# Flipped half tiles through DRAM in five transfers each, and two late features looked up from on-chip tables (recommender tower, one core)

## The chip, the cores and the metric

The kernel runs on one core of one Trainium2 chip. The metric is the device time of one execution in microseconds (us); less is better. The profile is one execution recorded by the hardware profiler.

## The reference

27 embedding tables are read by the ids of 2048 samples; all pairwise dot products of the 27 rows, with 16 dense inputs, go through three layers.

```python
e = jnp.stack([tbl_0[ids[:, 0]], ..., tbl_26[ids[:, 26]]], axis=1)   # (2048, 27, 128)
interactions = jnp.einsum('bnd,bmd->bnm', e, e)
i, j = jnp.triu_indices(27, k=1)
z = interactions[:, i, j]                                          # (2048, 351)
h = jnp.concatenate([z, dense_ctx], axis=1)                        # (2048, 367)
h = jnp.maximum(h @ W_top1 + b_top1, 0.0)                          # 512
h = jnp.maximum(h @ W_top2 + b_top2, 0.0)                          # 256
y = h @ W_top3
```

Tables have 1000, 1250, 12500 or 125000 rows. Those of features 24 and 25 have 1000.

## The kernel before

The samples are worked in 8 pairs p of tiles (t = 0, 1) of 128 samples each; a "cycle" below is the work of one pair on TensorE (PE). The product stage needs `emb` with the embedding dimension on the partitions, [dimension, tile, sample, feature]. Features get there in two ways.

**One-hot features** (11, each with 1000 rows). Their tables stay in SBUF in two rounded parts, `table_hi` and `table_lo`, 125 partitions by 8 chunks. VectorE (DVE) compares broadcast ids (`ids_b`) with row numbers and writes a "piece" of 125x2048 (`make_onehot`, line 798; a ring of 3 pieces). PE multiplies 16 times per piece pair: `look_up`, lines 625 and 627. ScalarE (ACT) takes the sums to `emb` and, for lookups that serve two pairs, to `held` (lines 923 and 924; placed one pair later by line 936). The set of 5 features is looked up in cycles 0, 2, 4, 6 and the set of 6 in cycles 1, 3, 5, always for two pairs at once (two pieces for a lookup; 8 matmuls of 512 columns per piece). Cycle 7 looks up 6 for itself alone, with one piece of 16 matmuls of 256 columns each.

**Gathered features** (16). GpSimd (POOL) issues one indirect DMA per feature and tile (line 596) into `rows`, a ring of 5 banks of 4 features. A tile has 4 banks n = 0 to 3. In pairs 1 to 7, three of the four half tiles (two banks each) are "flipped": DVE transposes 32x32 blocks (`flip_half`, line 853) into `flips`, SyncE's queue (SP) moves the blocks between partitions by DMA into `moved` (`move_half`, line 415: 4x4 transfers of 32 partitions by 1 KB, all issued one after another), and ACT copies `moved` to `emb` (`take_half`, line 955). The fourth half tile (t = 1, n = 2, 3) is transposed on PE (`turn`, line 636) between the products of tile 0 and layer 2.

`flips` and `moved` are single buffers. `flip_half` waits until the transfers of the half before have landed (line 848). `move_half` waits until its own half is flipped and until ACT has placed the half before (line 412).

**PE's order in cycle p**: the lookups of p; layer 1 of pair p-1 (`layer1`, line 672); products of tile 0 (`gram_products`, line 655); the two turned banks; layer 2 of p-1 (line 681); products of tile 1. After cycle 7 come the last pair's layers (`last_layers`).

**DVE's order in cycle p**: pieces 0, 1, 2; flip (p,0,0); the scores of p-2 (`score`, which wait for layer 2 in cycle p-1); piece 3; flip (p,0,1); pieces 4 to 7; flip (p,1,0); the rest of the pieces. In cycle 7 there are 6 pieces and the last flip follows them. The first part of this runs ahead, during PE's cycle p-1.

**ACT's order in cycle p**: place held; take half (p,0,0); take the lookups, with half (p,0,1) before the fifth; layer 1's four tiles; half (p,1,0); the products of tile 0; the two turned banks; the products of tile 1.

**SP's order in cycle p** (lines 515 to 532): up to two loads of ids, each of which waits until the piece of four lookups earlier is made; the four stores of the products of p-1 (line 440); move (p,0,1); the three loads of z (line 479), which wait for these stores; dense and ids; move (p,1,0); ids; move (p+1,0,0); store y. Products go out to DRAM in one layout and come back as z in another.

SP issues every one of these in this written order; a wait in it holds all that follows.

Of the kernel before, what the change touches and what calls it, by code (L numbers as in the profile page):

```python
# [31 lines left out]
F32 = mybir.dt.float32  # L32
# [5 lines left out]
P = 128  # L38
# [22 lines left out]

SETS = [list(range(NO // 2)), list(range(NO // 2, NO))]
HELD = max(len(features) for features in SETS)
LOOKUPS = [(0, 0, 2), (1, 0, 1), (1, 1, 2), (0, 2, 2), (1, 3, 2), (0, 4, 2), (1, 5, 2), (0, 6, 2), (1, 7, 1)]
IDS_SLOTS = 4


def emb_slot(k):
    return NG + k


def held_place(k):

    return k - SETS[1][0] if k in SETS[1] else k

# [11 lines left out]
def bank_features(p, n):  # L87

    end = min((n + 1) * TURNS_A_BANK, NG)
    return n * TURNS_A_BANK, end - n * TURNS_A_BANK  # L90
# [135 lines left out]
def build(nc, dense_t, ids_rows, ids_onehot, gathered_tables, onehot_tables, w1, w2, w3, b1, b2, out):  # L226
    with ExitStack() as ctx:
# [40 lines left out]
        products = nc.dram_tensor("products", (2, DRAM_ROWS, NF, QUARTERS, RUN), F32)  # L268

        last_products = nc.dram_tensor("last_products", (TILES, DRAM_ROWS, NF, QUARTERS, GROUPS), F32)  # L270

# [49 lines left out]
        turned = sem("turned")  # L321
        flipped = sem("flipped")
        half_moved = sem("half_moved")
        half_placed = sem("half_placed")
        emb_taken = sem("emb_taken")
        gram_full = sem("gram_full")
# [38 lines left out]

        HALF_MOVED = BLOCKS * BLOCKS * 16

# [23 lines left out]
        def _(sp):  # L391
            def load_ids(i):

                _, k, p0, pairs, _ = LOOKUP_LIST[i]
                if i - NO >= IDS_SLOTS:

                    sp.wait_ge(onehot_ready, pieces_by(i - IDS_SLOTS))
                slot = (i - NO) % IDS_SLOTS
                width = pairs * PAIR
                sp.dma_start(ids_b[:, slot, 0:width], ids_onehot[k:k + 1, p0 * PAIR:p0 * PAIR + width]  # L400
                             .rearrange("k b -> (k b)").partition_broadcast(P)).then_inc(ids_loaded[slot], 16)

            def lookups_of(p):
                return [i for i, lookup in enumerate(LOOKUP_LIST) if lookup[0] == p]

            def move_half(p, t, h):

                number = HALF_NUMBER[(p, t, h)]
                sp.wait_ge(flipped, FLIPPED_BY[(p, t, (h + 1) * HALF_BANKS - 1)])

                if number > 0:
                    sp.wait_ge(half_placed, number)
                for q in range(BLOCKS):
                    for b in range(BLOCKS):
                        sp.dma_start(  # L415
                            moved[b * BLOCK:(b + 1) * BLOCK, q, :, :].rearrange("p f j -> p (f j)"),
                            flips[q * BLOCK:(q + 1) * BLOCK, b, :, :, :].rearrange("p g f j -> p (g f j)")
                        ).then_inc(half_moved, 16)

# [88 lines left out]
            for dst, src in ((w1_sb[:], w1), (w2_sb[:], w2)):  # L508
                sp.dma_start(dst, src).then_inc(weights_loaded, 16)
            load_dense(0)  # L510
            for i in lookups_of(1)[:IDS_SLOTS]:
                load_ids(i)
            move_half(1, 0, 0)
# [88 lines left out]
        def _(pe):  # L602
# [7 lines left out]
            def look_up(i):  # L610
                _, k, p0, pairs, piece = LOOKUP_LIST[i]
                ps = free_emb_bank(("look", i))
                if i < NO:
                    pe.wait_ge(table_split, (k + 1) * GRAM_BANKS)
                chunks = ROWS_PER // pairs
                width = pairs * PAIR
                for part in range(pairs):
                    pe.wait_ge(onehot_ready, piece + part + 1)
                    if shared_onehot(i) and part == pairs - 1:

                        pe.wait_ge(onehot_rest, i + 1)
                    columns = onehot[0:ROWS, (piece + part) % ONEHOT_RING, :].rearrange("p (j b) -> p j b", b=width)
                    for c in range(chunks):
                        j = part * chunks + c
                        nc.tensor.matmul(ps[:, 0:width], table_hi[0:ROWS, k, j, :], columns[:, c, :],  # L625
                                         start=j == 0, stop=False)
                        last = nc.tensor.matmul(ps[:, 0:width], table_lo[0:ROWS, k, j, :], columns[:, c, :],  # L627
                                                start=False, stop=j == ROWS_PER - 1)
                    last.then_inc(onehot_read, 1)
# [145 lines left out]
        def _(dve):  # L775
# [67 lines left out]
            def flip_half(p, t, h):  # L843

                number = HALF_NUMBER[(p, t, h)]
                if number > 0:

                    dve.wait_ge(half_moved, number * HALF_MOVED)
                for g in range(HALF_BANKS):
# [4 lines left out]
                                        row_bank(p, t, n).rearrange("p f (b i) -> p f b i", b=BLOCKS)  # L854
                                        ).then_inc(flipped, 1)

            for p in range(1, PAIRS):
# [23 lines left out]
        def _(act):  # L881
# [66 lines left out]
            def take_half(p, t, h):  # L948
# [7 lines left out]
                               moved[:, :, 0:size, :].rearrange("d q f j -> d q j f")).then_inc(half_placed, 1)  # L956

            def take_gram(p, t):
                if t == 0 and p > 0:
# [42 lines left out]
            for p in range(PAIRS):  # L1002
# [21 lines left out]
                chunk = (p - 1) * MLP_CHUNKS  # L1024
                if p > 0:
                    for m in range(M1):
                        take_layer1(chunk, m)
                    take_half(p, 1, 0)
# [70 lines left out]
```

## Time and profile before

| | us |
|---|---|
| median of 3 runs | 444.68 (444.11 to 446.41) |
| the profiled execution, own time | 444.69 |
| its span, first to last instruction | 442.9 |
| TensorE busy | 341.5 (77%) |
| DVE busy | 246.3 (56%) |
| POOL busy | 242.6 (55%) |
| ACT busy | 199.4 (45%) |
| mean granted clock of TensorE | 0.903 of full |

Busy time leaves out DMA issue: SP's work is seen only in the chain that ended last, in the waits and in the timeline of its queue. In timeline rows the first number is the start in us from the beginning of the span, the second the duration; an idle time with what ended it stands in brackets. A row of windows gives the stretch, its length, the busy time (and instructions) of PE, PE's weight loads, DVE, ACT and POOL, then TensorE's granted clock as a share of full, the busy share of the DMA engines and GB/s. The starts of PE's cycles, T1 to T7, are where the first lookup of the pair runs.

### The profile page before, as it was taken

The numbers are of one execution on the slowest core, as the hardware profiler recorded it, in microseconds if no ns is written. First come the engines' busy times: TensorE is split into PE (matmuls) and PEld (weight loads), VectorE is DVE, ScalarE is ACT, GpSimd is POOL, SyncE is SP. The second block draws the span as 40 slices with busy tenths as digits, with TensorE's granted clock in tenths as the row PEclk, the third lists the DMA queues.
The fourth block names the chain that finished last, engine by engine and source line by source line (L and its number), as shares of the span: only waits on it lengthen the run. The fifth ranks groups of instructions, "written<-read, shape, count | busy, mean of one in ns | idle before, by whom it ended". The sixth has DMA issues, their size and how long they took to land.

```text
span 442.9 us, 8208 instructions
## 1 busy us (share of the span) xinstructions
PE 341.5 (77%) x3310; PEld 281.3 (64%) x3310; DVE 246.3 (56%) x202; ACT 199.4 (45%) x294; POOL 242.6 (55%) x263
## 2 busy tenths in 40 slices
PE   3999893759994989629896789809899489718767
PEld 2677793547872877428774678508786379717666
DVE  6899964596185726459266925739247743610100
ACT  5798663125463257113572166212662256322432
POOL 6777777660577637753377727754177737720000
PEclk9999998869999799959999699958999699867889
DMA  7966825562274536754174645844246533732230
GB/s 184 217 163 195 227 76 149 157 152 79 77 176 129 145 91 83 200 126 134 53 166 123 161 99 73 207 113 134 68 105 174 140 79 83 176 89 55 44 62 14
DMA packets 70111, 55.09 MB, mean 124 GB/s; under 512 B 45186, under 2 KB 60111, under 8 KB 70073
## 3 DMA queue, kind: packets, MB, share of 16 engines
q1 hardware_dynamic: 60121, 37.56, 35.4%
q0 software_dynamic: 8192, 16.79, 15.0%
q8 instruction: 26, 0.43, 0.4%
q10 hardware_dynamic: 1760, 0.22, 0.3%
q14 instruction: 12, 0.10, 0.1%
HBM read 36.43 MB, written 7.09 MB: 98 GB/s over the span
## 4 chain that ended last, share of the span: by engine, by line
SPq 45%; PE 30%; issue 10%; DMA 6%; DVE 5%; ACT 3%; ACTq 1%; DVEq 0%
SPq L415 31%; SPq L440 8%; PE emb_ps L625 7%; PE emb_ps L627 6%; PE mlp_ps L672 6%; DVE onehot L798 4%; PE gram_ps L655 4%; DMA moved<-flips 3%; DMA h<-tbl_rows 2%; PE mlp_ps L681 2%; SPq L400 2%; ACT emb L955 2%; PE emb_ps L699 1%; SPq L479 1%; DVE flips L853 1%
## 5 line engine op out<-in xcount | busy, mean ns | idle before, releaser
L596 POOL DMA_INDIRECT rows<-tbl_rows,idx x256 | 241.7, 944 | 147.5 <-issue 74.1
L625 PE MATMUL emb_ps<-onehot,table_hi 125*128 125x512 f32 (+1 forms) x400 | 158.0, 404 | 68.9 <-DVE onehot L798 59.5
L798 DVE TENSOR_TENSOR onehot<-ids_b,row_id 125x2048 fp32r<-125x2048 int32 x72 | 160.0, 2273 | 42.7 <-PE emb_ps L627 32.4
L627 PE MATMUL emb_ps<-onehot,table_lo 125*128 125x512 f32 (+1 forms) x400 | 152.1, 389 | 0.0
L625 PEld LDWEIGHTS emb_ps<-onehot,table_hi 125*128 125x128 f32 x400 | 82.5, 206 | 96.4 <-issue 59.1
L627 PEld LDWEIGHTS emb_ps<-onehot,table_lo 125*128 125x128 f32 x400 | 82.7, 207 | 13.0
L655 PE MATMUL gram_ps<-emb 128*54 128x54 f32 x2048 | 58.1, 216 | 11.2 <-ACT gram L966 10.2
L655 PEld LDWEIGHTS gram_ps<-emb 128*54 128x54 f32 x2048 | 54.9, 132 | 17.4 <-ACT gram L966 11.1
L955 ACT COPY emb<-moved 128x1024 f32<-128x1024 f32 x21 | 42.3, 2016 | 45.1 <-DMA moved<-flips 45.0
L853 DVE STREAM_TRANSPOSE flips<-rows 128x512 f32<-128x512 f32 x42 | 27.3, 689 | 62.0 <-DMA moved<-flips 62.0
L923 ACT COPY held<-emb_ps 128x256 f32<-128x256 f32 x38 | 14.2, 375 | 105.3 <-PE emb_ps L627 105.1
L966 ACT COPY gram<-gram_ps 118x432 f32<-118x432 f32 x64 | 32.5, 519 | 40.5 <-PE gram_ps L655 38.5
L672 PE MATMUL mlp_ps<-z,w_sb 126*128 126x256 f32 x168 | 40.3, 399 | 10.6 <-DMA z<-products 10.6
L672 PEld LDWEIGHTS mlp_ps<-z,w_sb 126*128 126x128 f32 x168 | 33.7, 201 | 16.2 <-DMA z<-products 10.8
L835 DVE TENSOR_TENSOR mlp_ps<-mlp_ps,rows 128x256 f32<-128x256 f32 x14 | 6.1, 433 | 65.4 <-PE mlp_ps L681 65.4
L924 ACT COPY emb<-emb_ps 128x256 f32<-128x256 f32 x50 | 33.7, 688 | 5.8 <-PE emb_ps L627 5.8
L798 DVE TENSOR_TENSOR onehot<-z,mlp_ps 125x2048 fp32r<-125x2048 int32 (+1 forms) x16 | 33.5, 2116 | 1.5 <-PE mlp_ps L726 1.1
L681 PE MATMUL mlp_ps<-w_sb,h 128*128 128x256 f32 x112 | 25.3, 379 | 0.0
L975 ACT ACTIVATE h<-mlp_ps,columns 128x256 f32<-128x256 f32 x28 | 13.3, 474 | 24.1 <-PE mlp_ps L672 24.1
L681 PEld LDWEIGHTS mlp_ps<-w_sb,h 128*128 128x128 f32 x112 | 20.7, 190 | 2.5
L936 ACT COPY emb<-held 128x1280 f32<-128x1280 f32 (+1 forms) x7 | 19.2, 2739 | 0.2
L945 ACT COPY emb<-emb_ps 128x512 f32<-128x512 f32 x22 | 13.6, 652 | 0.1
(51 smaller groups left out, 129.0 us busy)
## 6 DMA issues: line engine op xcount, KB each, us to landing
moved<-flips SPq DMA_DIRECT2D x336, 32.0 KB
ids_b<-ids_onehot SPq DMA_DIRECT2D x33, 256.0 KB, 4.7
products<-gram SPq DMA_DIRECT2D x28, 216.0 KB
gram<-tbl_rows SPq DMA_DIRECT2D x9, 480.0 KB
rows<-tbl_rows,idx POOLq DMA_INDIRECT x256
z<-products SPq DMA_DIRECT2D x14, 126.0 KB
h<-tbl_rows SPq DMA_DIRECT2D x2, 480.0 KB
z<-products SPq DMA_DIRECT2D x7, 112.0 KB
```

Of the source, the lines that this page charges most:

```text
L415: sp.dma_start(moved[b * BLOCK:(b + 1) * BLOCK, q, :, :].rearrange("p f j -> p (f j)"), flips[q * BLOCK:(q + 1) * BLOCK, b, :, :, :].rearr ...
L440: sp.dma_start(products[p % 2, to:to + STORE_ROWS, :, q, :], gram[row:end, q % ABREAST, :, :]).then_inc(products_out, 16)
L596: pool.indirect_dma_start(out=rows[:, bank_number(p, t, n) % ROW_BANKS, f - first, :], out_offset=None, in_=gathered_tables[f], in_offset= ...
L625: nc.tensor.matmul(ps[:, 0:width], table_hi[0:ROWS, k, j, :], columns[:, c, :], start=j == 0, stop=False)
L627: last = nc.tensor.matmul(ps[:, 0:width], table_lo[0:ROWS, k, j, :], columns[:, c, :], start=False, stop=j == ROWS_PER - 1)
L655: last = nc.tensor.matmul(ps[half * HALF_ROWS:half * HALF_ROWS + GRAM_COLS, b * GRAM_COLS:(b + 1) * GRAM_COLS], samples, samples, start=Tr ...
L672: last = nc.tensor.matmul(ps[:, 0:PAIR], w1_sb[0:k, s, m * P:(m + 1) * P], z[0:k, s, :], start=s == 0, stop=s == STEPS - 1)
L681: last = nc.tensor.matmul(mlp_ps[t][:, 0:HID2], h1[:, k, t * P:(t + 1) * P], w2_sb[:, k, :], start=k == 0, stop=k == M1 - 1)
L798: nc.vector.tensor_tensor(onehot[0:ROWS, seq % ONEHOT_RING, 0:own * width].rearrange("p (j b) -> p j b", b=width), *operands, ALU.is_equal ...
L924: nc.scalar.copy(emb[:, :, :, emb_slot(k)], ps[:, 0:PAIR].rearrange("d (t b) -> d t b", t=TILES)).then_inc(emb_taken, 1)
L955: nc.scalar.copy(emb[:, t, :, first:first + size].rearrange("d (q j) f -> d q j f", j=BLOCK), moved[:, :, 0:size, :].rearrange("d q f j -> ...
L966: nc.scalar.copy(gram[0:GRAM_PART, :, :, g0:g0 + GROUPS_A_BANK].rearrange("r s j g -> r (s j) g"), gram_ps[a % GRAM_BANKS][0:GRAM_PART, 0: ...
```

## The change

1. `move_half` is split. `store_half` waits for the flip and writes the whole of `flips` (128 partitions by 4 KB) to a DRAM tensor `halves` in one transfer. `load_half` waits for that transfer to land and for ACT to have placed the half before, and reads `moved` back with four transfers of 32 partitions by 4 runs of 1 KB. `flip_half` now waits for the store of the half before, no longer for `moved`. `halves` has two places. In SP's order the store of (p,0,1) stands before the loads of z and its load behind them; (p,1,0) has one load of ids between store and load; (p+1,0,0) has nothing between.
2. Features 24 and 25, the last two gathered ones, are looked up one-hot for pairs 6 and 7. Bank 3 of these tiles shrinks from 4 features to 2. Cycle 6 gets two more lookups (4 pieces). Their tables go into the places of one-hot tables 0 and 1 after the last lookup of those: SP loads each through `h1` as stage (`load_late_table`), ACT rounds it (`round_late`), DVE forms the low part (`split_late`). SP loads table 1 only after the split of table 0. Their ids come from `ids_rows`, copied within DRAM by four transfers of 4-byte elements near the start (`store_late_ids`).

```diff
+LATE_FEATURES = [24, 25]
+LATE_SLOT = GATHERED.index(LATE_FEATURES[0])
+LATE_PAIR = PAIRS - 2
...
+LATE_SPLITS = [6, 9]
 HALF_AFTER = 4
+LATE_ROUNDS = [2, 4]
...
+            def store_half(p, t, h):
+                sp.wait_ge(flipped, FLIPPED_BY[(p, t, (h + 1) * HALF_BANKS - 1)])
                 number = HALF_NUMBER[(p, t, h)]
-                sp.wait_ge(flipped, FLIPPED_BY[(p, t, (h + 1) * HALF_BANKS - 1)])
+                sp.dma_start(halves[number % 2], flips[:, :, :, :, :].rearrange("p b g f j -> p b (g f j)")
+                             ).then_inc(half_stored, 16)
+
+            def load_half(p, t, h):
+                number = HALF_NUMBER[(p, t, h)]
+                sp.wait_ge(half_stored, (number + 1) * 16)
                 if number > 0:
                     sp.wait_ge(half_placed, number)
-                for q in range(BLOCKS):
-                    for b in range(BLOCKS):
+                for b in range(BLOCKS):
+                    sp.dma_start(moved[b * BLOCK:(b + 1) * BLOCK, :, :, :].rearrange("p q f j -> p q (f j)"),
+                                 halves[number % 2, :, b, :].rearrange("(q p) x -> p q x", p=BLOCK)
+                                 ).then_inc(half_moved, 16)
+            def store_late_ids():
+                for n in range(len(LATE)):
+                    for t in range(TILES):
                         sp.dma_start(
+                            late_ids[n:n + 1, :].rearrange("k (p t b) -> t (k p) b", t=TILES, b=P)[t],
+                            ids_rows[LATE_PAIR:PAIRS, :, :].rearrange(
+                                "a p (t f) -> f t a p", t=TILES)[LATE_SLOT + n, t],
+                            allow_slow_non_contiguous=True).then_inc(late_ids_stored, 16)
+            def load_late_table(n):
+                if n == 0:
+                    sp.wait_ge(mlp_full, (LATE_PAIR - 1) * MLP_CHUNKS)
+                else:
+                    sp.wait_ge(late_split, n)
...
             for p in range(1, PAIRS):
+                if p == LATE_PAIR:
+                    load_late_table(0)
                 for i in ids[0:2]:
                     load_ids(i)
                 store_products(p - 1)
-                move_half(p, 0, 1)
+                store_half(p, 0, 1)
+                if p == LATE_PAIR:
+                    load_late_table(1)
                 load_z(p - 1)
+                load_half(p, 0, 1)
                 load_dense(p)
...
-                move_half(p, 1, 0)
-                for i in ahead[2:]:
+                store_half(p, 1, 0)
+                for i in ahead[2:3]:
+                    load_ids(i)
+                load_half(p, 1, 0)
+                for i in ahead[3:]:
                     load_ids(i)
                 if p < LAST:
-                    move_half(p + 1, 0, 0)
+                    store_half(p + 1, 0, 0)
+                    load_half(p + 1, 0, 0)
                     store_y(p - 1)
...
                 if number > 0:
-                    dve.wait_ge(half_moved, number * HALF_MOVED)
+                    dve.wait_ge(half_stored, number * 16)
...
+            def split_late(n):
+                dve.wait_ge(late_rounded, n + 1)
+                nc.vector.tensor_tensor(table_lo[...], late_stage, table_hi[...].bitcast(F32), ALU.subtract
+                                        ).then_inc(late_split, 1)
...
+                    if p == LATE_PAIR and at in LATE_SPLITS:
+                        split_late(LATE_SPLITS.index(at))
                     make_onehot(i, part)
...
+            def round_late(n):
+                act.wait_ge(late_loaded, (n + 1) * 16 * len(TABLE_PARTS))
+                act.wait_ge(onehot_read, pieces_by(cycle_lookups(LATE_PAIR)[n]))
+                nc.scalar.copy(table_hi[...], late_stage).then_inc(late_rounded, 1)
...
                     if p > 0 and at == HALF_AFTER:
                         take_half(p, 0, 1)
+                    if p == LATE_PAIR and at in LATE_ROUNDS:
+                        round_late(LATE_ROUNDS.index(at))
```

## Rows read from the trace of the kernel before

**Rows 1.** The chain that ended last, as shares of the span, by engine and line.

```profile
SPq 45%; PE 30%; issue 10%; DMA 6%; DVE 5%; ACT 3%; ACTq 1%; DVEq 0%
SPq L415 31%; SPq L440 8%; PE emb_ps L625 7%; PE emb_ps L627 6%; PE mlp_ps L672 6%; DVE onehot L798 4%; PE gram_ps L655 4%; DMA moved<-flips 3%; DMA h<-tbl_rows 2%; PE mlp_ps L681 2%; SPq L400 2%; ACT emb L955 2%; PE emb_ps L699 1%; SPq L479 1%; DVE flips L853 1%
```

**Rows 2.** Windows: cycles 1 to 7 and the tail (columns: see the section on the profile).

```profile
62.40:121.00 58.60, 43.58 (x401) 35.99 (x400) 32.08 (x24) 21.15 (x31) 32.11 (x35) 0.88 0.45 121
121.00:168.00 47.00, 38.88 (x389) 31.41 (x385) 27.78 (x22) 21.50 (x30) 30.02 (x32) 0.93 0.54 134
168.00:223.50 55.50, 41.73 (x403) 33.84 (x401) 31.99 (x24) 21.78 (x31) 30.11 (x33) 0.88 0.53 119
223.50:270.10 46.60, 38.90 (x388) 31.50 (x384) 27.78 (x22) 21.30 (x29) 30.18 (x33) 0.93 0.55 135
270.10:326.20 56.10, 42.06 (x405) 34.03 (x401) 31.99 (x24) 21.74 (x31) 30.47 (x33) 0.88 0.52 118
326.20:373.00 46.80, 38.54 (x387) 31.13 (x385) 27.78 (x22) 21.30 (x29) 29.94 (x32) 0.93 0.49 120
373.00:423.60 50.60, 34.03 (x404) 30.98 (x400) 11.23 (x13) 18.76 (x24) 13.50 (x15) 0.80 0.37 87
423.60:442.90 19.30, 12.03 (x74) 10.79 (x70) 0.98 (x4) 4.12 (x12) 0.00 (x0) 0.91 0.21 40
```

**Rows 3.** Timeline of SP's queue, cycles 3 and 4.

```profile
172.85 7.01 SPq L440 DMA_DIRECT2D products<-gram  x4
179.96 11.20 SPq L415 DMA_DIRECT2D moved<-flips  x16
...
225.69 4.86 SPq L440 DMA_DIRECT2D products<-gram  x4
230.65 10.40 SPq L415 DMA_DIRECT2D moved<-flips  x16
241.14 2.58 SPq L479 DMA_DIRECT2D z<-products  x3
```

**Rows 4.** Timeline of DVE, cycles 3 and 4.

```profile
192.89 1.30 DVE L853 STREAM_TRANSPOSE flips<-rows 128x512 f32<-128x512 f32 x2 [10.46 <-DMA moved<-flips]
...
229.14 8.84 DVE L798 TENSOR_TENSOR onehot<-ids_b,row_id 125x2048 fp32r<-125x2048 int32 x4
242.36 1.30 DVE L853 STREAM_TRANSPOSE flips<-rows 128x512 f32<-128x512 f32 x2 [4.38 <-DMA moved<-flips]
```

**Rows 5.** Timeline of PE: starts of matmuls in cycle 4, and its layer 1.

```profile
226.35 0.39 PE L625 MATMUL emb_ps<-onehot,table_hi 125*128 125x512 f32 x1
226.57 0.39 PE L627 MATMUL emb_ps<-onehot,table_lo 125*128 125x512 f32 x1
...
245.98 0.77 PE L625 MATMUL emb_ps<-onehot,table_hi 125*128 125x512 f32 x1 [5.83 <-DVE onehot L798]
...
252.30 5.36 PE L672 MATMUL mlp_ps<-z,w_sb 126*128 126x256 f32 x24
```

**Rows 6.** Windows within cycle 4, before and after PE's idle time that ends at 245.98.

```profile
224.00:240.00 16.00, 15.27 (x63) 11.16 (x62) 12.27 (x7) 8.09 (x9) 12.27 (x13) 1.00 0.66 158
246.00:251.20 5.20, 5.20 (x12) 4.12 (x13) 4.61 (x3) 0.00 (x0) 3.98 (x5) 0.50 0.77 196
```

**Rows 7.** Timeline of POOL in cycle 4: two gathers, the first behind a turned bank.

```profile
263.20 0.94 POOL L596 DMA_INDIRECT rows<-tbl_rows,idx  x1 [6.97 <-PE emb_ps L636]
264.45 0.94 POOL L596 DMA_INDIRECT rows<-tbl_rows,idx  x1 [0.31 <-issue]
```

**Rows 8.** DMA landings: ids of 256 KB (source view of line 400) and `moved` (chain).

```profile
DMA to landing us min/median/max: 3.8/4.5/10.2
...
407.79 2.67 DMA moved<-flips
```

**Rows 9.** Groups by form (busy us, mean ns): low parts of tables, halves taken.

```profile
L819 DVE TENSOR_TENSOR table_lo<-gram,gram_ps 125x512 fp32r<-125x512 f32 x18 | 11.5, 681 | 1.1 <-ACT gram_ps L896 1.1
L955 ACT COPY emb<-moved 128x1024 f32<-128x1024 f32 x21 | 42.3, 2016 | 45.1 <-DMA moved<-flips 45.0
```

More of the change, by code:

```diff
@@ L58 @@
 ONEHOT_RING = 3
-SETS = [list(range(NO // 2)), list(range(NO // 2, NO))]
-HELD = max(len(features) for features in SETS)
-LOOKUPS = [(0, 0, 2), (1, 0, 1), (1, 1, 2), (0, 2, 2), (1, 3, 2), (0, 4, 2), (1, 5, 2), (0, 6, 2), (1, 7, 1)]
+LATE_FEATURES = [24, 25]
+LATE_SLOT = GATHERED.index(LATE_FEATURES[0])
+LATE_PAIR = PAIRS - 2
+LATE = [NO + n for n in range(len(LATE_FEATURES))]
+SETS = [list(range(NO // 2)), list(range(NO // 2, NO)), LATE]
+LOOKUPS = [(0, 0, 2), (1, 0, 1), (1, 1, 2), (0, 2, 2), (1, 3, 2), (0, 4, 2), (1, 5, 2), (0, 6, 2),
+           (2, LATE_PAIR, 2), (1, 7, 1)]
+HELD = len(LATE) + len(SETS[0])
 IDS_SLOTS = 4
 def emb_slot(k):
-    return NG + k
+    return NG + k if k < NO else LATE_SLOT + k - NO
 def held_place(k):
-    return k - SETS[1][0] if k in SETS[1] else k
+    first = SETS[1][0] if k in SETS[1] else LATE_SLOT - NG
+    return (k if k < NO else emb_slot(k) - NG) - first
 EMB_BANKS = 3
@@ L87, in bank_features @@
 def bank_features(p, n):
-    end = min((n + 1) * TURNS_A_BANK, NG)
+    end = min((n + 1) * TURNS_A_BANK, LATE_SLOT if p >= LATE_PAIR else NG)
     return n * TURNS_A_BANK, end - n * TURNS_A_BANK
@@ L268, in build @@
         products = nc.dram_tensor("products", (2, DRAM_ROWS, NF, QUARTERS, RUN), F32)
+        halves = nc.dram_tensor("halves", (2, P, BLOCKS, HALF_BANKS * TURNS_A_BANK * BLOCK), F32)
+        late_ids = nc.dram_tensor("late_ids", (len(LATE), 2 * PAIR), I32)
+        late_stage = h1[0:ROWS, :, :].rearrange("p m b -> p (m b)")
         last_products = nc.dram_tensor("last_products", (TILES, DRAM_ROWS, NF, QUARTERS, GROUPS), F32)
@@ L322, in build @@
         flipped = sem("flipped")
+        half_stored = sem("half_stored")
         half_moved = sem("half_moved")
         half_placed = sem("half_placed")
+        late_ids_stored = sem("late_ids_stored")
+        late_loaded = sem("late_loaded")
+        late_rounded = sem("late_rounded")
+        late_split = sem("late_split")
         emb_taken = sem("emb_taken")
@@ L399, in load_ids @@
                 width = pairs * PAIR
-                sp.dma_start(ids_b[:, slot, 0:width], ids_onehot[k:k + 1, p0 * PAIR:p0 * PAIR + width]
-                             .rearrange("k b -> (k b)").partition_broadcast(P)).then_inc(ids_loaded[slot], 16)
+                if k >= NO:
+                    sp.wait_ge(late_ids_stored, len(LATE) * TILES * 16)
+                    ids = late_ids[k - NO:k - NO + 1, :]
+                else:
+                    ids = ids_onehot[k:k + 1, p0 * PAIR:p0 * PAIR + width]
@@ L420, in load_dense @@
+            def load_late_table(n):
+                if n == 0:
+                    sp.wait_ge(mlp_full, (LATE_PAIR - 1) * MLP_CHUNKS)
+                else:
+                    sp.wait_ge(late_split, n)
+                table = gathered_tables[LATE_SLOT + n].rearrange("(p j) d -> p (j d)", j=ROWS_PER)
+                for p0, p1 in TABLE_PARTS:
+                    sp.dma_start(late_stage[p0:p1, :], table[p0:p1, :]).then_inc(late_loaded, 16)
             def load_dense(p):
@@ L614, in look_up @@
                     pe.wait_ge(table_split, (k + 1) * GRAM_BANKS)
+                if k in LATE:
+                    pe.wait_ge(late_split, k - NO + 1)
+                table = k % NO
                 chunks = ROWS_PER // pairs
@@ L624, in look_up @@
                         j = part * chunks + c
-                        nc.tensor.matmul(ps[:, 0:width], table_hi[0:ROWS, k, j, :], columns[:, c, :],
+                        nc.tensor.matmul(ps[:, 0:width], table_hi[0:ROWS, table, j, :], columns[:, c, :],
                                          start=j == 0, stop=False)
-                        last = nc.tensor.matmul(ps[:, 0:width], table_lo[0:ROWS, k, j, :], columns[:, c, :],
+                        last = nc.tensor.matmul(ps[:, 0:width], table_lo[0:ROWS, table, j, :], columns[:, c, :],
                                                 start=False, stop=j == ROWS_PER - 1)
@@ L1025, in _ @@
                 if p > 0:
+                    if p == LATE_PAIR:
+                        act.wait_ge(late_split, len(LATE))
                     for m in range(M1):
```

17 lines of the change are left out of this document (11 added, 6 removed).

## The prediction

> **What bounds the kernel now.** I read the chain that ended last first [rows 1]. SP's queue holds 45% of it, and the block transfers of line 415 alone 31%: the path runs through the issue of small transfers, more than through arithmetic. Next come the windows by cycle [rows 2]. TensorE is busy 39 to 44 us of each cycle of 47 to 58 us, at a granted clock of 0.88 to 0.93. So there are idle stretches, and a clock that falls with them. SP's timeline shows their source [rows 3]: in cycle 4 the stores of products take until 230.55, the 16 transfers of half (4,0,1) start only then and are issued for 10.40 us. DVE wants to flip (4,1,0) after its pieces, at 238.0, and waits 4.38 us for them [rows 4]. PE then idles 5.83 us at 245.98 [rows 5]. The granted clock is 1.00 in the stretch before and 0.50 in the 5.2 us behind it, that is 2.4 GHz and then 1.2 GHz [rows 6]: 12 matmuls there take 0.43 us each, against 0.22 to 0.24 before [rows 5, 6]. In odd cycles SP starts the stores of products later (172.85 is T3 + 4.9, since the second load of ids waits for piece 3; 225.69 is T4 + 2.2), they take 7.01 us, and DVE waits 10.46 us [rows 3, 4]. POOL issues one gather per 1.25 us [rows 7], 40 us for 32 of them. It is free of the path now, but not by much once cycles shrink.
>
> **What a cycle costs when no half tile is waited for.** From cycle 4: DVE starts pieces 4 to 7 at 229.14, T4 + 5.6, and a piece takes 8.84 / 4 = 2.21 us, longer than PE's 8 matmuls (8 x 0.23 = 1.84) [rows 4, 5]. They end at T + 14.5, the flip takes 1.2 us, pieces 8 and 9 end at T + 20.1, and PE is through them at T + 22.2 (1.84 and a quarter of a us to start). From layer 1 to the next cycle it takes 270.1 - 252.30 = 17.8 us [rows 2, 5]. That makes 40.0 us for an even cycle. An odd one has two pieces more: 40.0 + 4.4 = 44.4 us. This DVE-paced walk holds only if three covers hold.
>
> **Part 1, the halves.** Sixteen issues (10.4 us) become one store and four loads. The nearest rows for one issue are 0.65 us (line 415) and 0.86 (line 479, whose transfers have more runs) [rows 3]; I take 0.6, so 3 us of issue. But there are two landings in a row now. No row shows a 512 KB leg to or from DRAM. Bounds for a leg are 2.7 us (32 KB, SBUF to SBUF) and the median 4.5 us and maximum 10.2 us of ids loads of 256 KB [rows 8]. I take 4.0 us for the store, nearer the ids, and 2 to 2.5 us behind the last issue for the four loads. The Trainium skill (DMA: Bandwidth & Descriptors, Anatomy of one DMA) puts about 2 us of fixed cost, mostly the write receipt, on a transfer, plus bytes / 436 GB/s: an estimate of 3.2 us for this store, and the forecast would be some 3 us lower by it.
> - Even cycle (2, 4), SP: products from T + 0.7 to 5.6 (SP is free earlier than before); store (p,0,1) right behind, landed T + 10.3. DVE asks for `flips` at T + 14.5: covered by 4 us. The stored products have landed by about T + 9, z is issued to 11.6, the load of the half to 14.1, landed 16.5, and ACT has placed it by T + 19 (2.0 us [rows 9]), before layer 1 at T + 22.2. Half (p,1,0) is stored at 16.4, loaded by T + 25; ACT wants it at 27.6. Nothing is late: 40.0 us.
> - Odd cycle (1, 3, 5): ids hold SP until T + 4.9, products take 5 to 7 us, store (p,0,1) is issued at T + 10.5 to 12.4 and lands at T + 14.5 to 16.5. DVE is held 0 to 2 us. I take +1.5 in cycles 3 and 5 and +0.6 in cycle 1, so 45.0, 45.9, 45.9 us.
> - Without stalls over 1.2 us on PE I expect the granted clock near 1.00. This is in the 17.8 us and 1.84 us already.
>
> Behind the store's wait on SP stand z, dense and ids; all have 4 us or more. POOL's 32 gathers (40 us) just fit an even cycle and turn into a wait of about 0. The other readers of the gathers have about 5 us of room. The single buffers are reused later than they come free, in each case by the same order of ACT.
>
> **Part 2, the late features.** Removed: 8 gathers (10 us of POOL, beside other work, worth nothing on the path) and 4 PE transposes (under 1 us). Added in cycle 6: 4 pieces, 4 x 2.21 = 8.8 us on the DVE pace; two splits of 125x1024, bounded below by one group of 0.68 and above by two, 1.36 [rows 9]; I take 1.2 each, 2.4 us. Two ACT roundings are covered. Then there is a new wait. SP's order in cycle 6 is: ids until T + 4.9 (the fifth and sixth lookup, as in an odd cycle), products to T + 11, store (6,0,1), table 1 (its stage is free at T + 11.4), z to T + 17, load (6,0,1) to T + 19.5, landed T + 22. ACT takes the half first (to T + 24) and only then rounds table 1 (to T + 25). DVE wants its split before piece 9, at T + 19 to 20, and waits 5 to 6 us; the 5 pieces behind it queue up. The split ends at T + 26.3, five pieces take 11, PE is done at T + 39.4. PE has idled some 7 us, and as behind the 5.83 us [rows 5, 6] I add a slow clock, +0.8 net of what DVE's pace hides: T + 40.2. Cycle 6: 40.2 + 17.8 = 58 us, where 46.8 stood. So part 2 costs about 18 us against the 40.0 that cycle 6 would take without it.
>
> The four copies of late ids (1024 elements of 4 bytes) go before the ids of cycle 1. No row shows their like. They cost between nothing and 3 us in cycle 1: these ids are wanted some 10 us before PE reads the pieces. I take 0. The Trainium skill (same page, Why a DMA increments its semaphore by 16 and not by 1) says that a transfer runs on as many engines as divide its slowest dimension, here 2 of 16; the forecast would be up to 3 us higher by it.
>
> **Cycle 7.** Before, 50.6 us, with DVE and PE behind SP twice. Now: 6 pieces of 16 short matmuls are done at T + 12; z arrives at T + 13 (stores of products until T + 5.7, then z); half (7,0,1) is placed at T + 18 and holds ACT, and with it PE's third tile of layer 1, by 3 to 4 us; half (7,1,0) is placed at T + 25, then products, turned banks, layer 2 and products end at T + 35.5. With slow clock after these stalls 37 us. If all transfers came in time it would be 12.1 + 19.3, the sum of PE's work, 31.4.
>
> **The sum.** T1 = 62.4 and the tail of 19.3 stay [rows 2]. 62.4 + 45.0 + 40.0 + 45.9 + 40.0 + 45.9 + 58 + 37 + 19.3 = 393.5 us of span. The profiled execution took 444.69 for a span of 442.9, so 1.8 are added: 395.3, rounded to 395.5. The profiled execution is the median of the runs (444.68), so no shift is made.
>
> **Rivals.**
> 1. *All covers hold.* Legs land as soon as the 2.7 us row says, odd cycles take 44.4, cycle 6 has no wait at the split (22.2 + 8.8 + 2.4 + 17.8 = 51.2), cycle 7 takes 31.4. Then 62.4 + 44.4 x 3 + 80 + 51.2 + 31.4 + 19.3 + 1.8 = 379.3. For it: the issue time that goes is three times what is left. Against it: SP's order in cycle 6 puts two landings and z ahead of the rounding. 0.15.
> 2. *Legs of 6 to 7 us under load.* The DMA engines are already at a share of 0.66 to 0.77 in cycle 4 [rows 6], and each half now moves twice the bytes; ids have taken 10.2 us [rows 8]. Odd cycles +3 to 4.5 (with the clock behind each stall), cycle 6 +5, cycle 7 +5: 395.5 + 12 + 10 = 417. 0.20.
> 3. *Slower than before: SP blocked on its own stores.* It now waits for a landing before each load. Per cycle SP has about 19 us of issue and 4 landings in line (three stores, the products before z). That is 19 + 4L; it equals today's mean cycle (361.2 / 7 = 51.6 us [rows 2]) at L = 8.2 us, and decides from there on; at the maximum of 10.2 [rows 8] a cycle would take 60 us and the kernel 420 + 83.5 = 503; with half of the cycles so bad, (503 + 395.5) / 2 = 449. Against: the median leg is 4.5. 0.04.
> 4. *It changes nothing*, as DVE, POOL and PE refill the gaps: it would need cycles of 51.6 us bound elsewhere; POOL needs 40, DVE 28 to 32 busy [rows 2]. 0.02.
>
> **How the numbers follow.** Forecast 0.59 (387 to 404), rival 1 0.15, rival 2 0.20, rival 3 0.04, rival 4 0.02. The range 378 to 414 leaves out the slower half of rival 2, rivals 3 and 4, and little of rival 1. A measurement of this kernel tells some 0.5% from no change. Faster 0.95, same 0.01, slower 0.04.
>
> **What would show it.** In the profile after: no wait of DVE's flips for a transfer in even cycles, up to 2 us in odd ones; cycles of about 40 and 45 us; SP's line for products among the largest of SP; a DVE wait of 5 to 6 us for ACT's rounding at the second split, and cycle 6 the longest of all; POOL waiting a few us per cycle. Wrong would be: PE's idle time before line 625 still near 60 us; a store that lands after more than 6 us; a slow clock in even cycles.

## The result, and the profile after

The changed kernel takes 417.94 us (median of 3 runs, 416.65 to 420.86) against 444.68. The ratio is 0.940, with a 95% interval of 0.932 to 0.949: 27 us faster. The forecast was 395.5 us with a range of 378 to 414. The direction was right, the time lies above the range.

Where it lies is seen at once when the windows by cycle are set beside those of [rows 2]. The first row is the start of the kernel up to T1, then cycles 1 to 7 and the tail; columns as there.

```profile
0.00:68.40 68.40, 54.64 (x488) 43.52 (x488) 46.91 (x42) 47.77 (x78) 50.05 (x59) 0.98 0.79 152
68.40:134.30 65.90, 44.62 (x400) 36.79 (x400) 39.87 (x29) 21.45 (x31) 28.02 (x30) 0.82 0.63 155
134.30:174.20 39.90, 36.63 (x388) 29.47 (x384) 27.62 (x22) 21.19 (x29) 30.14 (x33) 1.00 0.79 197
174.20:219.00 44.80, 40.80 (x404) 32.32 (x400) 31.99 (x24) 21.84 (x31) 30.24 (x33) 1.00 0.72 183
219.00:258.90 39.90, 36.64 (x390) 29.46 (x384) 27.62 (x22) 21.19 (x29) 30.14 (x33) 1.00 0.74 199
258.90:303.20 44.30, 40.85 (x406) 32.32 (x400) 31.90 (x24) 21.77 (x31) 30.29 (x33) 1.00 0.73 183
303.20:361.50 58.30, 45.77 (x418) 36.80 (x414) 38.39 (x28) 24.28 (x35) 26.47 (x29) 0.91 0.57 149
361.50:398.20 36.70, 30.62 (x402) 27.45 (x398) 10.66 (x13) 18.85 (x24) 9.95 (x11) 0.95 0.55 135
398.20:416.10 17.90, 11.95 (x70) 10.79 (x70) 0.98 (x4) 4.01 (x12) 0.00 (x0) 0.89 0.22 42
```

| stretch | before | forecast | after |
|---|---|---|---|
| to T1 | 62.4 | 62.4 | 68.4 |
| cycle 1 | 58.6 | 45.0 | 65.9 |
| cycle 2 | 47.0 | 40.0 | 39.9 |
| cycle 3 | 55.5 | 45.9 | 44.8 |
| cycle 4 | 46.6 | 40.0 | 39.9 |
| cycle 5 | 56.1 | 45.9 | 44.3 |
| cycle 6 | 46.8 | 58 | 58.3 |
| cycle 7 | 50.6 | 37 | 36.7 |
| tail | 19.3 | 19.3 | 17.9 |

Cycles 2 to 7 came as worked out, within 1.6 us each. The start and cycle 1 are 26.9 us longer than forecast. Cycle 1 is even 7.3 us longer than before the change. (A cycle starts here where the products before it end. PE's first lookup of cycle 1 runs only at 82.95, so the stop ahead of it counts in cycle 1.) So the question is what happened between 40 and 100 us. The timeline of SP's queue, same columns as [rows 3]:

```profile
40.45 20.92 SPq L452 DMA_DIRECT2D late_ids<-ids_rows  x4
61.42 13.34 SPq L423 DMA_DIRECT2D ids_b<-ids_onehot  x4
88.44 0.33 SPq L433 DMA_DIRECT2D halves<-flips  x1
91.31 1.85 SPq L444 DMA_DIRECT2D moved<-halves  x4
...
224.79 0.33 SPq L433 DMA_DIRECT2D halves<-flips  x1
...
230.36 1.91 SPq L444 DMA_DIRECT2D moved<-halves  x4
```

The four copies of late ids (line 452) hold SP for 20.92 us, and the four loads of ids behind them for 13.34 us, where they took 2.5 us in the kernel before. The chain that ended last, in order of time, and the timelines of DVE and PE show who pays:

```profile
41.26 4.88 SPq L452
...
46.18 6.19 SPq L452
...
52.41 8.97 SPq L452
...
61.42 19.07 DMA ids_b<-ids_onehot
```

```profile
80.51 6.68 DVE L861 TENSOR_TENSOR onehot<-ids_b,row_id 125x2048 fp32r<-125x2048 int32 x3 [28.61 <-DMA ids_b<-ids_onehot]
...
188.92 1.31 DVE L916 STREAM_TRANSPOSE flips<-rows 128x512 f32<-128x512 f32 x2 [0.21 <-DMA halves<-flips]
...
233.45 1.29 DVE L916 STREAM_TRANSPOSE flips<-rows 128x512 f32<-128x512 f32 x2
...
329.14 1.23 DVE L923 TENSOR_TENSOR table_lo<-h,table_hi 125x1024 fp32r<-125x1024 f32 x1 [7.19 <-ACT table_hi L1035]
```

```profile
82.95 0.76 PE L688 MATMUL emb_ps<-onehot,table_hi 125*128 125x512 f32 x1 [14.57 <-DVE onehot L861]
```

Each copy takes longer to issue than the one before (0.76, 4.88, 6.19, 8.97 us). The first load of ids lands 19.07 us after its issue; DVE, which wants it at 51.9, waits 28.61 us, and PE stops for 14.57 us. The 6 us ahead of T1 lie in PE's products of pair 0: they take 13.5 us (54.89 to 68.4) where the kernel before takes 7.0, with gaps that wait for nothing the profile shows (last section) and a granted clock of 0.57 from 64 to 68 us. The waits that were the kernel's bound are gone: DVE waited 4.38 and 10.46 us for the transfers of a half in cycles 4 and 3 [rows 4], and waits nothing and 0.21 us now. In the chain, SP's share went from 45% [rows 1] to 12%:

```profile
PE 47%; DMA 17%; SPq 12%; DVE 10%; issue 9%; ACT 4%; ACTq 0%; DVEq 0%
```

### The profile page after: what moved, and what is told of

The parts are those of the page before. It is cut to its first block, busy times and chain, and to the rows that moved or that the text cites. A ratio compares the mean times of both kernels' runs of the same rounds, so it can differ in the third digit from the quotient of the medians.

```text
span 416.1 us, 8058 instructions
## 1 busy us (share of the span) xinstructions
PE 342.5 (82%) x3338; PEld 278.9 (67%) x3338; DVE 255.9 (62%) x208; ACT 202.3 (49%) x300; POOL 235.3 (57%) x255
## 4 chain that ended last, share of the span: by engine, by line
PE 47%; DMA 17%; SPq 12%; DVE 10%; issue 9%; ACT 4%; ACTq 0%; DVEq 0%
PE emb_ps L688 11%; PE emb_ps L690 10%; PE gram_ps L718 9%; DVE onehot L861 8%; PE mlp_ps L735 7%; PE mlp_ps L744 6%; SPq L452 5%; DMA ids_b<-ids_onehot 5%; DMA products<-gram 4%; DMA moved<-halves 4%; DMA halves<-flips 3%; DMA h<-tbl_rows 2%; PE emb_ps L699 2%; SPq L489 2%; SPq L528 2%
## 5 line engine op out<-in xcount | busy, mean ns | idle before, releaser
L656 POOL DMA_INDIRECT rows<-tbl_rows,idx x248 | 234.5, 945 | 138.5 <-issue 72.2
L861 DVE TENSOR_TENSOR onehot<-ids_b,row_id 125x2048 fp32r<-125x2048 int32 x76 | 168.5, 2272 | 56.1 <-DMA ids_b<-ids_onehot 28.6
L688 PE MATMUL emb_ps<-onehot,table_hi 125*128 125x512 f32 (+1 forms) x416 | 159.2, 392 | 47.4 <-DVE onehot L861 40.3
L718 PE MATMUL gram_ps<-emb 128*54 128x54 f32 x2048 | 59.3, 216 | 12.6 <-ACT gram L1046 8.4
L1027 ACT COPY emb<-moved 128x1024 f32<-128x1024 f32 (+1 forms) x21 | 42.3, 2015 | 47.9 <-DMA moved<-halves 47.6
L996 ACT COPY emb<-emb_ps 128x256 f32<-128x256 f32 x52 | 35.1, 688 | 4.3 <-PE emb_ps L690 4.3
L916 DVE STREAM_TRANSPOSE flips<-rows 128x512 f32<-128x512 f32 (+1 forms) x42 | 26.9, 675 | 7.5 <-DMA rows<-tbl_rows,idx 4.1
L1008 ACT COPY emb<-held 128x1280 f32<-128x1280 f32 (+2 forms) x7 | 20.0, 2854 | 0.2
L968 ACT COPY gram_ps<-table_hi 125x512 f32<-125x512 f32 x22 | 13.3, 645 | 0.1
```

The source lines that it names most:

```text
L656: pool.indirect_dma_start(out=rows[:, bank_number(p, t, n) % ROW_BANKS, f - first, :], out_offset=None, in_=gathered_tables[f], in_offset= ...
L688: nc.tensor.matmul(ps[:, 0:width], table_hi[0:ROWS, table, j, :], columns[:, c, :], start=j == 0, stop=False)
L718: last = nc.tensor.matmul(ps[half * HALF_ROWS:half * HALF_ROWS + GRAM_COLS, b * GRAM_COLS:(b + 1) * GRAM_COLS], samples, samples, start=Tr ...
L861: nc.vector.tensor_tensor(onehot[0:ROWS, seq % ONEHOT_RING, 0:own * width].rearrange("p (j b) -> p j b", b=width), *operands, ALU.is_equal ...
L916: nc.vector.transpose(flips[:, :, g, 0:size, :].rearrange("p b f j -> p f b j"), row_bank(p, t, n).rearrange("p f (b i) -> p f b i", b=BLOCKS)
L996: nc.scalar.copy(emb[:, :, :, emb_slot(k)], ps[:, 0:PAIR].rearrange("d (t b) -> d t b", t=TILES)).then_inc(emb_taken, 1)
```

## The experiments

The theory after the result has three parts. (1) The copies of late ids are the whole of the miss, because only 2 of the 16 DMA engines run them (which the trace does not name; what speaks for it stands at the second experiment). (2) The halves' new way earns some 70 us, by fewer issues and by the early release of `flips`. (3) The late features cost some 18 us. The rivals stand in each expectation. Ratios are to runs of the kernel before on the same chip.

### The late ids as an input

```diff
-            store_late_ids()
             for i in lookups_of(1)[:IDS_SLOTS]:
...
-                    sp.wait_ge(late_ids_stored, len(LATE) * TILES * 16)
-                    ids = late_ids[k - NO:k - NO + 1, :]
+                    ids = ids_late[k - NO:k - NO + 1, :]
...
+        dram("ids_late", ids[LATE_PAIR * PAIR:, LATE_FEATURES].T),
```

> The changed kernel without the four copies of late ids within DRAM: the late ids come laid out as an input of their own, as those of the other one-hot features do. Theory A (the copies of 4-byte elements hold SP's queue and the DMA engines, and through them the first ids of cycle 1): T1 goes back from 68.4 to 62.4, cycle 1 from 65.9 to about 45, the other cycles stay as in the changed kernel (39.9, 44.8, 39.9, 44.3, 58.3, 36.6, tail 17.9), so 389.1 of span and 391 us. Rival B (the long cycle 1 comes from the halves' way through DRAM beside the loads of that time): no more than the 6 us at the start come back, 410 us or more.

Measured: 389.5 us, ratio 0.877 (0.871 to 0.882). The copies cost 28 us. T1 is back at 62.3 and cycle 1 takes 44.4 us at full clock, as its row of windows shows:

```profile
62.30:106.70 44.40, 40.94 (x406) 32.38 (x401) 32.01 (x24) 21.58 (x31) 32.13 (x35) 1.00 0.75 202
```

The halves' way through DRAM beside the loads of that time is not to blame.

### The same copies over more engines

```diff
-late_ids[n:n + 1, :].rearrange("k (p t b) -> t (k p) b", t=TILES, b=P)[t],
+late_ids[n:n + 1, :].rearrange("k (p t b) -> t b (k p)", t=TILES, b=P)[t],
-ids_rows[LATE_PAIR:PAIRS, :, :].rearrange("a p (t f) -> f t a p", t=TILES)[LATE_SLOT + n, t],
+ids_rows[LATE_PAIR:PAIRS, :, :].rearrange("a p (t f) -> f t p a", t=TILES)[LATE_SLOT + n, t],
```

> The changed kernel with the same four copies, the same 1024 elements of 4 bytes, but with the two axes of each copy exchanged, so that the slowest one has 128 elements and not 2. Theory A1 (the price is that of a transfer run by 2 of the 16 DMA engines; the rule is that of the Trainium skill, DMA: Bandwidth & Descriptors, Why a DMA increments its semaphore by 16 and not by 1): each engine gets an eighth of the elements, SP issues the four within 4 us and the kernel takes 391 to 395 us. Rival A2 (the price is per element or per copy, however it is spread): SP still takes about 20 us for the four, 415 to 418 us.

Measured: 390.8 us, ratio 0.879 (0.874 to 0.884). SP's queue:

```profile
41.31 4.42 SPq L452 DMA_DIRECT2D late_ids<-ids_rows  x4
45.77 2.03 SPq L423 DMA_DIRECT2D ids_b<-ids_onehot  x4
```

The same 1024 elements of 4 bytes, to and from the same places, now take 4.42 us of issue instead of 20.92, and the kernel stands 1.3 us above the one without copies. Only the order of the two axes changed. So neither the count nor the size of the elements made the price, but how each copy is laid out. The rule of the Trainium skill (DMA: Bandwidth & Descriptors, Why a DMA increments its semaphore by 16 and not by 1) says that the engines used are the largest number up to 16 that divides the slowest dimension of both sides: 2 before the edit and 16 after. The two runs agree with it.

The trace does not name the engine of a packet, but its count of packets bears on the 2 and the 16. The pages of the changed kernel, of the one with the ids as an input and of this one say:

```profile
DMA packets 70455, 67.10 MB, mean 161 GB/s; under 512 B 42466, under 2 KB 57391, under 8 KB 70419
DMA packets 69423, 67.10 MB, mean 173 GB/s; under 512 B 41434, under 2 KB 56359, under 8 KB 69387
DMA packets 70511, 67.10 MB, mean 173 GB/s; under 512 B 42522, under 2 KB 57447, under 8 KB 70475
```

Against the version without copies, the four copies bring 1032 packets in the changed kernel and 1088 here: 1024 elements, and 2 packets more per copy in the first case, 16 in the second. Other transfers of these kernels bring 16 more than their data: 21 added stores of 128 rows (in the experiment on the store leg) bring 3025 packets, and 21 x (128 + 16) is 3024. One closing packet for each engine in use would give these 2 and 16; that this is what they are is inferred.

### The copies behind the ids

```diff
-            store_late_ids()
             for i in lookups_of(1)[:IDS_SLOTS]:
                 load_ids(i)
+            store_late_ids()
             store_half(1, 0, 0)
```

> The changed kernel with the four copies of late ids issued behind the four loads of ids of cycle 1, not ahead of them. Theory A (two engines work through 512 elements each for some 38 us, and whatever is issued behind waits for these two engines): the ids are in time, but half (1,0,0), stored at about 66, lands only when the two engines are through, at about 82; PE stops in cycle 1 when its banks are full; 405 to 410 us. Rival (the harm was that the ids stood behind the copies in SP's issue order): 392 to 396 us.

Measured: 420.2 us, ratio 0.943 (0.937 to 0.950), as slow as the changed kernel. My theory's sign was right and its size too small by 10 us. SP's queue, DVE and ACT:

```profile
44.28 26.44 SPq L452 DMA_DIRECT2D late_ids<-ids_rows  x4
71.06 9.18 SPq L433 DMA_DIRECT2D halves<-flips  x1
91.91 1.77 SPq L444 DMA_DIRECT2D moved<-halves  x4
```

```profile
70.32 0.71 DVE L916 STREAM_TRANSPOSE flips<-rows 128x512 f32<-128x512 f32 x1 [8.56 <-DMA rows<-tbl_rows,idx]
```

```profile
96.47 2.07 ACT L1027 COPY emb<-moved 128x1024 f32<-128x1024 f32 x1 [19.94 <-DMA moved<-halves]
```

The ids are in time, but the first store of a half is stuck for 9.18 us in issue and lands at 91.9. DVE also waits 8.56 us for a gather of POOL, which is issued on another queue. The chain that ended last runs through both landings:

```profile
51.62 18.68 DMA rows<-tbl_rows,idx
...
71.06 20.83 DMA halves<-flips
```

So the harm was not only that the ids stood behind the copies in SP's order: behind the copies a store on SP's queue and a gather on POOL's landed late too. That the gathers suffer is the part that I had left out.

### Part 1 alone

```diff
-           (2, LATE_PAIR, 2), (1, 7, 1)]
+           (1, 7, 1)]
-    end = min((n + 1) * TURNS_A_BANK, LATE_SLOT if p >= LATE_PAIR else NG)
+    end = min((n + 1) * TURNS_A_BANK, NG)
...
-            store_late_ids()
-                if p == LATE_PAIR:
-                    load_late_table(0)
```

and the same for the second table, both roundings and both splits.

> Part 1 alone: halves through DRAM in five transfers, features 24 and 25 gathered for all pairs as before, no late ids, tables, splits or roundings. Theory A with the late features a loss of 18 us: cycle 6 as cycle 4 (39.9 for 58.3), the rest as expected without the copies, 391 - 18.4 = 372.5 us. Rival C (POOL is the bound once SP is not, and the late features earn more than they cost): cycles 6 and 7 grow by the 10 us of 8 more gathers, 385 us or more.

Measured: 372.4 us, ratio 0.835 (0.828 to 0.843), the fastest version. Cycle 6 (275.1 to 315.0), beside the 58.3 us above:

```profile
275.10:315.00 39.90, 36.69 (x385) 29.48 (x386) 27.62 (x22) 21.12 (x29) 30.15 (x33) 1.00 0.70 185
315.00:352.40 37.40, 31.02 (x400) 27.59 (x400) 11.03 (x13) 18.59 (x24) 13.43 (x15) 0.95 0.56 138
```

With 32 gathers in each of the last pairs cycle 6 takes 39.9 us and cycle 7 0.7 us more than after. The 8 gathers that the late features save were on no path. A second set of runs, beside two other versions, gave the same:

> Halves only once more, unchanged, on the chip of the two runs beside it, for their comparison: 369 to 376 us, as in its first run, even cycles 39.9 us, odd ones 44.3.

Measured: 373.8 us, ratio 0.843 (0.838 to 0.848).

### Part 2 alone

The late features with their ids as an input, and the halves moved by the 16 transfers of `move_half`; DVE waits for them as before.

> Part 2 alone: the halves move by the 16 transfers of the kernel before, features 24 and 25 are looked up late, their ids come as an input. Theory A (the late lookups cost DVE and PE time in cycle 6 and take only POOL time that nobody waits for): cycle 6 goes from 46.8 to 56 to 58 us, cycle 7 stays within 2 us of 50.6, about 455 us, slower than before. Rival (with SP as the bound, DVE and PE have room and the added pieces hide in it): 440 to 446 us.

Measured: 450.3 us, ratio 1.011 (1.0045 to 1.018): slower than before, by 1.1%. Cycles 6 and 7:

```profile
321.80:380.90 59.10, 46.41 (x414) 35.92 (x414) 38.59 (x28) 24.29 (x35) 27.29 (x28) 0.91 0.47 118
380.90:428.80 47.90, 31.23 (x409) 28.15 (x404) 10.88 (x13) 19.56 (x25) 9.95 (x11) 0.86 0.35 85
```

Cycle 6 takes 59.1 us for 46.8, cycle 7 47.9 for 50.6 [rows 2]. That is +9.6 us where I expected +10, but the span of the profiled execution grew by 5.5 us only (448.4 for 442.9): cycles 1 to 5, whose work the edit leaves as it is, take 259.7 us together in this trace, for 263.8. Why they are shorter stays open. The sign holds: part 2 does not pay with SP as the bound either.

### The second rounding ahead of the half

```diff
-                    if p > 0 and at == HALF_AFTER:
-                        take_half(p, 0, 1)
                     if p == LATE_PAIR and at in LATE_ROUNDS:
                         round_late(LATE_ROUNDS.index(at))
+                    if p > 0 and at == HALF_AFTER:
+                        take_half(p, 0, 1)
```

> The changed kernel without the copies of late ids (late ids as an input), and in cycle 6 ACT rounds table 1 before it takes half (6,0,1), not after. Theory A (the second split waits in ACT's queue behind the half): DVE's wait at the second split falls from 7.2 us to 2 or less, cycle 6 from 58.3 to about 53, 386 us. Rival D (the load of table 1 on SP's queue ends last anyway): cycle 6 stays at 57 to 58 and the time at 391 us.

Measured: 383.4 us, ratio 0.864 (0.858 to 0.870), 6 us below the version with the ids as an input. DVE at the second split, and cycle 6:

```profile
295.42 1.23 DVE L921 TENSOR_TENSOR table_lo<-h,table_hi 125x1024 fp32r<-125x1024 f32 x1 [0.65 <-ACT table_hi L1033]
```

```profile
276.10:327.30 51.20, 44.81 (x416) 34.94 (x415) 38.39 (x28) 24.21 (x35) 27.42 (x29) 1.00 0.68 170
```

The wait falls from 7.19 to 0.65 us, cycle 6 from 58.3 to 51.2, and the granted clock in it rises from 0.91 to 1.00. The 51.2 us are what rival 1 of the prediction worked out for a cycle 6 without the wait. Even so the late features cost 11 us against part 1 alone.

### Part 1 taken apart: the early release, the number of issues

```diff
-                    dve.wait_ge(half_stored, number * 16)
+                    dve.wait_ge(half_moved, number * HALF_MOVED)
```

> Halves only, five transfers each, but DVE waits again, as in the kernel before, until the half before has landed in its second buffer, not only until it is stored in DRAM. It keeps the small number of issues and takes away the early release of the first buffer. Theory A (both count; half (p,0,1) lands at about T + 17 in even and T + 21 in odd cycles, and DVE wants its buffer at T + 14.5): even cycles 43 us, odd cycles 52, 372.4 + 3 x 8 + 3 x 3 + 3 = 408 us. Rival (the gain is the issue count alone, the early release is idle): 373 to 377 us.

Measured: 411.0 us, ratio 0.927 (0.924 to 0.930). In the profiled execution, the shortest of its five (405.7 us), cycles 4 and 5 take 44.1 and 51.3 us, where 43 and 52 were expected. DVE in these cycles:

```profile
226.14 1.30 DVE L911 STREAM_TRANSPOSE flips<-rows 128x512 f32<-128x512 f32 x2 [2.69 <-DMA moved<-halves]
...
273.62 1.30 DVE L911 STREAM_TRANSPOSE flips<-rows 128x512 f32<-128x512 f32 x2 [6.24 <-DMA moved<-halves]
```

The next one keeps the early release and brings back 16 issues:

```diff
-                for b in range(BLOCKS):
-                    sp.dma_start(moved[b * BLOCK:(b + 1) * BLOCK, :, :, :].rearrange("p q f j -> p q (f j)"),
-                                 halves[number % 2, :, b, :].rearrange("(q p) x -> p q x", p=BLOCK)
+                for q in range(BLOCKS):
+                    for b in range(BLOCKS):
+                        sp.dma_start(moved[b * BLOCK:(b + 1) * BLOCK, q, :, :].rearrange("p f j -> p (f j)"),
+                                     halves[number % 2, q * BLOCK:(q + 1) * BLOCK, b, :]
```

> Halves only with the early release, but the half comes back in 16 transfers of 32 partitions by 1 KB, as many as in the kernel before. Theory A (both count; SP gets 12 x 0.6 = 7.5 us more issue per half, 22 us per cycle, and half (p,0,1) reaches ACT after layer 1 should start): even cycles 45 us, odd cycles 48 to 50, 372.4 + 3 x 5 + 3 x 5 + 5 = 407 us. Rival (once DVE waits for the store alone, the issues are hidden): 373 to 378 us.

Measured: 449.2 us, ratio 1.007 (1.002 to 1.0125): nothing is left of the gain. Both theories were too low, mine by 42 us. SP's queue and ACT in cycle 4:

```profile
237.59 8.28 SPq L445 DMA_DIRECT2D moved<-halves  x16
...
253.87 7.30 SPq L445 DMA_DIRECT2D moved<-halves  x16
```

```profile
262.56 1.92 ACT L1021 COPY emb<-moved 128x1024 f32<-128x1024 f32 x1 [7.86 <-DMA moved<-halves]
```

I had followed half (p,0,1) only. Here half (p,1,0) is on the path. ACT has placed (4,0,1) by 249.8, but the store of (4,1,0), issued at 247.32 right behind the 16 transfers, lands only after 6.53 us (the chain: `247.32 6.53 DMA halves<-flips`); the load behind it takes 7.30 us of issue, and the products of tile 0 stand behind it in ACT's queue. DVE waits for a half for 5.8 us in the whole kernel, ACT for 107. So the many small transfers cost twice: by their own issue (17% of the chain) and by stores that land late behind them (12%); these runs do not part the two. Against 373.8 us on the same chip, the small number of transfers is worth 75 us given the early release, and the early release 37 us given the small number. They are not a sum: each alone leaves the other's wait in place.

### The cover of the store leg

```diff
-                sp.dma_start(halves[number % 2], flips[...]).then_inc(half_stored, 16)
+                for copy in range(2):
+                    sp.dma_start(halves[2 * copy + number % 2], flips[...]).then_inc(half_stored, 16)
```

with both waits for `half_stored` raised to 32 per half.

> Halves only (part 1 alone), but each half is stored twice, to two places in DRAM, and both stores must have landed where one had to. This doubles the bytes of the store leg. Theory A (the store leg has 4 us of cover in even cycles and next to none in odd ones, where DVE waited 0.2 us for it): even cycles stay at 39.9 us, odd cycles grow by 1.5 to 2.5 us each, cycle 7 by 2, so 372.4 + 8 = 380 us. Rival (the DMA engines' bandwidth is what is short): even cycles grow as well, 388 us or more. Rival (all is covered): 372 to 374 us.

Measured: 384.2 us, ratio 0.859 (0.852 to 0.865), 10 to 12 us more than part 1 alone (373.8 and 372.4, on other chips), for 21 more stores of 512 KB. The profiled execution was the longest of its runs (386.7), so its cycles say little beyond their order: 48.1, 42.4, 46.2, 40.4, 46.7 and 39.9 us for cycles 1 to 6. DVE waits for the store 3.46, 1.49 and 1.76 us in the three odd cycles and not at all in the even ones, as theory A has it. The time stands between theory A (380) and the first rival (388): cycle 2 grew as well, by 2.5 us, and no row of DVE explains it. There is little cover to give away in odd cycles.

### The half ahead of z in cycle 7

```diff
+                if p == LAST:
+                    load_half(p, 0, 1)
                 load_z(p - 1)
-                load_half(p, 0, 1)
+                if p < LAST:
+                    load_half(p, 0, 1)
```

> Halves only, and in cycle 7 SP issues the loads of half (7,0,1) before the loads of z, which wait for the stored products. Theory A (in cycle 7 ACT waits 8.2 us for this half, and lookups and layer 1 stand behind it): that wait ends 4 to 5 us earlier, PE's stop of 3.3 us within layer 1 goes, cycle 7 falls from 37.5 to about 33 us, 368 us. Rival (z then comes later by as much, and PE waits for it before layer 1): 371 to 373 us.

Measured: 374.5 us, ratio 0.840 (0.835 to 0.844), no different from part 1 alone. The rival was right. PE in cycle 7 of part 1 alone, and then here:

```profile
329.23 2.86 PE L730 MATMUL mlp_ps<-z,w_sb 126*128 126x256 f32 x12 [1.90 <-DMA z<-products]
335.38 4.52 PE L730 MATMUL mlp_ps<-z,w_sb 126*128 126x256 f32 x12 [3.29 <-ACT h L1048]
```

```profile
334.37 7.54 PE L733 MATMUL mlp_ps<-z,w_sb 126*128 126x256 f32 x24 [5.34 <-DMA z<-products]
```

Two stops of 1.90 and 3.29 us turned into one of 5.34. Which of the two transfers goes first does not matter here, since layer 1 needs both.

## Why the prediction was wrong, point by point

- **The bound (SP's small transfers): right.** SP's share of the chain fell from 45% to 12%, and bringing the 16 transfers back (449.2 us) gives the old time, by their issue and by the stores that land late behind them. The range of 39 to 44 us for TensorE's busy time and of 0.88 to 0.93 for its clock leaves out cycle 7 (34.0 us at 0.80 [rows 2]).
- **A cycle on DVE's pace, 40.0 and 44.4 us: right.** 39.9 and 44.3 to 44.8 were measured, at a granted clock of 1.00, from a 17.8 us stretch and a 2.21 us piece.
- **The legs of the round trip: one size does not fit them, and no leg decided the time.** I took 4.0 us for every store. The first one, in cycle 1, landed in 2.85 us (the chain: `88.44 2.85 DMA halves<-flips`). That is nearer to the estimate of 3.2 us worked out from the Trainium skill (DMA: Bandwidth & Descriptors, Anatomy of one DMA), which gives its figures for transfers issued by GpSimd; this store is issued by SP. But the store of (3,1,0), with a load of a half and loads of ids just ahead of it, took 7.63 us (the chain: `193.72 7.63 DMA halves<-flips`). This is the sign that I had named as wrong, a store that lands after more than 6 us. It cost little: cycle 3 took 44.8 us where cycle 5 took 44.3. The 1.5 us that I added to cycles 3 and 5 did not come; DVE waited 0.21 us.
- **The late features cost 18 us: right.** 389.5 with and 372.4 without are 17 us. The wait at the second split was 7.19 us where 5 to 6 were worked out, and for the reason given, as the edit of the order showed.
- **Cycle 7 in 37 us: right** (36.7), with the two stops on PE that were named, 1.08 us for z and 2.90 us for ACT within layer 1.
- **The copies of late ids at nothing, with 3 us as the upper end: this is the step that failed.** They cost 28 us (417.9 against 389.5 without them). I bounded them by the slack of the ids (wanted 10 us before PE reads the pieces), and never by their own length. No row of the kernel before showed transfers of single elements, and such a case calls for a bound from the nearest price per packet on the fewest engines, not from the slack of one reader. I had the rule on the 2 engines and gave it 3 us, because I counted the delay of one load and not what the copies do to SP's issue, to the stores of halves and to POOL's gathers. The 28 us minus what the odd cycles and the tail gave back (some 4 to 5 us) make the 22 us between 395.5 and 417.9.
- **Rival 2 (slow legs under load) gave 417 us and was not what happened.** The time fits by chance: a leg of 7.63 us did occur in cycle 3, but cycles 2 to 7 came within 1.6 us of the forecast, and the loss stands in the start and in cycle 1.
- **The other sign:** PE's idle time behind DVE's pieces fell from 59.5 us to 40.3, of which 14.6 are the one stop of cycle 1; the granted clock was 1.00 in cycles 2 and 4 and 0.91 in cycle 6, behind the wait at the split.

## What to carry to other kernels

A transfer whose slowest axis has only 2 entries can block far more than its bytes: here, exchanging the axes (2 entries to 128) or taking the data as an input took its cost from 28 us to 1.3 and to nothing. Bound what no row shows by its own length on the fewest engines before asking who waits for it. Where a queue was bound by many small transfers, even a detour through DRAM with a landing in the middle was cheaper (372.4 us for 444), once the wait for the first buffer was moved to the first leg (411.0 without that); and work taken from an engine that was on no path (POOL's gathers, turned into lookups) was paid by those that were: 17 us, of which the order of ACT's work made 6.

## What the runs showed of the hardware

- The issue time of a transfer on SP's queue is no constant: 0.76 to 8.97 us for the same copy, and 13.34 us for four loads of ids (10.55 of it one of them) that take 2.03 us behind spread copies. One store of 512 KB took 9.18 us of issue behind the copies; in the changed kernel such stores take 0.33 to 1.25 us. Each of these long issues stands behind transfers that were slow to finish; that SP is held until these drain is inferred.
- If 2 engines ran the copies, as the counts of packets suggest, each had 512 elements of 4 bytes. From the first issue at 40.45 to the landing of the first ids behind them at 80.49 it is 40 us, or about 78 ns per element, an estimate from above: other transfers stood ahead of them, and no row names an engine.
- The landing of a 512 KB store of a half took 2.85 us in cycle 1, 7.63 us behind other transfers in cycle 3, and 20.83 us behind the copies.
- Transfers on the other queue suffered with them: a gather that DVE waited 8.56 us for had taken 18.68 us to land. PE also shows gaps within its products between 58 and 65 us (1.08 and 1.10 us the longest) that wait for nothing the profile shows; the kernel with the ids as an input has none. In the changed kernel a packet on an instruction queue starts at 58.07 and takes 2.92 us, where such packets take at most 1.42 us between 50 and 80 us in the kernel before and in the two versions without the slow copies. That such packets made the gaps is not shown.
